# Perceiver block with 12,544 keys on one core: a dot product of the similarities moved from TensorE to VectorE, the centred input transposed in the head, hq's first half transposed sooner

## What is computed

```python
# 1: cross attention, enc = layernorm(x), decoder_hq = ctx
Sim = (enc @ w1)[:, :, None] + (ctx @ w2)[:, None, :] + einsum(enc * w3, ctx) + b_sim[0]
A = softmax(Sim, axis=2)
hq_hat = A @ ctx
Batt = softmax(max(Sim, axis=2), axis=1)
hc_bar = Batt @ enc
feats = concat([enc, hq_hat, enc * hq_hat, enc * hc_bar])
x = x + feats @ W_qv + b_qv
# 2: x = x + attn(layernorm(x))      (16 heads, rotary, no softmax)
# 3: x = x + ffn(layernorm(x))
```

## Time and profile before

| | |
|---|---|
| time of 3 runs | 112.22 us median (112.09 to 112.31) |
| the profiled execution | 112.1 us, of which 110.3 us are the span from the first to the last instruction |
| granted TensorE clock, mean over the span | 1.0 of full |
| PE busy | 105.1 us (95%), 582 matmuls |
| DVE busy | 93.1 us (84%) |
| ACT busy | 82.4 us (75%) |
| POOL busy | 29.3 us (27%) |
| DMA | 29.82 MB, mean 270 GB/s over the span |

### The profile page before, as it was taken

One profiled execution on the slowest core, in us unless ns is written; L12 is line 12 of the kernel. 1 busy time (PEld: TensorE's weight loads), 2 busy tenths in 40 slices (PEclk: granted clock), 3 DMA queues, 4 the chain that ended last, 5 costly groups with the idle time before them and its releaser, 6 DMA issues.

```text
span 110.3 us, 1855 instructions
## 1 busy us (share of the span) xinstructions
PE 105.1 (95%) x582; PEld 86.4 (78%) x583; DVE 93.1 (84%) x152; ACT 82.4 (75%) x171; POOL 29.3 (27%) x47
## 2 busy tenths in 40 slices
PE   5999999999999999999999999999999998998890
PEld 2368768588858888899899999989898997887680
DVE  1478999999998998999999999999999847674352
ACT  5067668899979989999999899988976725903450
POOL 2239200444043314233242424286330000200100
PEclk9999999999999999999999999999999999999999
DMA  2999999999999999999999999960000000000001
GB/s 72 367 406 423 416 422 422 416 422 422 409 420 417 418 415 423 417 420 442 442 389 423 415 422 425 406 260 0 3 0 0 0 6 0 0 0 0 6 3 48
DMA packets 8220, 29.82 MB, mean 270 GB/s; under 512 B 1042, under 2 KB 1298, under 8 KB 8082
## 3 DMA queue, kind: packets, MB, share of 16 engines
q1 hardware_dynamic: 8064, 29.69, 66.3%
q10 hardware_dynamic: 146, 0.01, 0.1%
HBM read 29.57 MB, written 0.13 MB: 269 GB/s over the span
## 4 chain that ended last, share of the span: by engine, by line
PE 94%; DVE 1%; issue 1%; ACT 1%; DVEq 0%; ACTq 0%
PE mixed_ps L997 18%; PE scores_ps L968 10%; PE mixed_ps L999 9%; PE scores_ps L940 8%; PE scores_ps L944 8%; PE scores_ps L954 8%; PE scores_ps L925 7%; PE scores_ps L910 4%; PE scores_ps L979 3%; PE scores_ps L1090 2%; PE mixed_ps L1142 2%; PE side_ps L1016 1%; PE scores_ps L1155 1%; PE side_ps L1133 1%; PE scores_ps L1016 1%; PE scores_ps L1125 1%
## 5 line engine op out<-in xcount | busy, mean ns | idle before, releaser
L698 DVE TENSOR_TENSOR pair<-raw,pair 128x1024 fp32r<-128x1024 f32 (+2 forms) x42 | 49.0, 1183 | 1.3 <-ACT pair L488 1.0
L488 ACT ACTIVATE pair<-raw 128x512 fp32r<-128x512 f32 (+1 forms) x42 | 34.5, 820 | 3.8 <-DMA raw<-keys_dram 3.4
L997 PE MATMUL mixed_ps<-pair,turned_high 128*128 128x512 f32 x84 | 32.3, 418 | 0.0
L999 PE MATMUL mixed_ps<-pair,turned_low 128*128 128x256 f32 x84 | 23.6, 281 | 0.0
L463 POOL CAST pair<-raw 128x512 fp32r<-128x512 f32 x22 | 13.6, 619 | 27.3 <-DVE pair L698 23.1
L997 PEld LDWEIGHTS mixed_ps<-pair,turned_high 128*128 128x128 f32 x84 | 15.8, 188 | 2.8
L520 ACT ACTIVATE turned_high<-scores_ps 128x512 fp32r<-128x512 f32 (+1 forms) x23 | 13.4, 584 | 4.0 <-PE scores_ps L968 4.0
L721 DVE TENSOR_SCALAR_CACHE_REDUCE neg_scores<-scores_ps,neg_max 128x1024 f32<-128x1024 f32 (+1 forms) x13 | 15.8, 1216 | 0.2
L999 PEld LDWEIGHTS mixed_ps<-pair,turned_low 128*128 128x128 f32 x84 | 16.0, 190 | 0.0
L728 DVE TENSOR_TENSOR turned_low<-scores_ps,turned_high 128x512 fp32r<-128x512 f32 (+1 forms) x23 | 15.3, 667 | 0.2 <-ACT turned_high L520 0.2
L968 PE MATMUL scores_ps<-ident,neg_scores 128*128 128x128 f32 x98 | 14.6, 272 | 0.0
(11 more groups left out here) (189 smaller groups left out, 130.6 us busy)
## 6 DMA issues: line engine op xcount, KB each, us to landing
raw<-keys_dram SPq DMA_DIRECT2D x24, 512.0 KB, 10.0
raw<-rows_dram SPq DMA_DIRECT2D x24, 512.0 KB, 9.2
w<-weights_dram SPq DMA_DIRECT2D x1, 1792.0 KB, 9.9
w<-weights_dram SPq DMA_DIRECT2D x2, 512.0 KB, 10.4
const<-const_dram SPq DMA_DIRECT2D x1, 832.0 KB, 11.5
raw<-keys_last_dram SPq DMA_DIRECT2D x1, 256.0 KB, 10.2
raw<-rows_last_dram SPq DMA_DIRECT2D x1, 256.0 KB, 6.8
x_sb<-x_dram SPq DMA_DIRECT2D x1, 128.0 KB, 2.2
```

What stands on the lines that cost most here:

```text
L488: nc.scalar.activation(pair[:, use % PAIR_BUFS, 0, 0:columns], raw[:, slot(item), 0:columns], ACT.Copy)\
L698: nc.vector.tensor_tensor(out=pair[:, use % PAIR_BUFS, 1, 0:columns], in0=raw[:, slot(item), 0:columns], in1=pair[:, use % PAIR_BUFS, 0, 0 ...
L997: nc.tensor.matmul(mixed_ps[:, :].rearrange("p (h d) -> p h d", h=2), probs_high, both[:, :, t * D:(t + 1) * D], start=(k == EARLY and t = ...
L999: last = nc.tensor.matmul(mixed_ps[:, 0:D], probs_low, rows_tile(high, t), start=False, stop=(k == LATE - 1 and end))
```

## The change

Three things are changed. First, `hw1` is no longer made by PE: SP loads w1 and `b_sim`, repeated in all 128 partitions (128 x 257 numbers, 1028 bytes in a row), behind chunk 14; DVE multiplies `normed` with it and sums along the row in one instruction ahead of the low half of chunk 19; `b_sim` is added in the instruction that makes `sim_max`. The small transfer of `b_sim` on ACT's queue goes. Second, ACT makes `x_c` in the head, before the query's high half; PE transposes it there (one warm-up matmul fewer), ACT copies the two halves to `x_c_t` behind the high half of chunk 3, and DVE adds `x_c_t` and the bias where x1 leaves PSUM, now for both halves; ACT squares the low half from there. Third, at the seam the first half of `hq` is transposed ahead of the last product with `normed_t` instead of behind two, the second behind it.

```diff
-WARM_START, WARM_NORM_2, WARM_SHIFT = 9, 2, 2
+WARM_START, WARM_NORM_2, WARM_SHIFT = 8, 2, 2
...
-        x_c = sb("x_c", [P, D])
+        x_c = neg_scores[:, S - 2 * D:S - D]
+        x_c_t = sb("x_c_t", [P, DH, P])
...
+        x_c_turn_ps = (banks[5][:, 0:P], banks[5][:, P:2 * P])
...
+                if k == 14:
+                    sp.dma_start(w1_rows[:, :], w1_rows_in).then_inc(w1_rows_loaded, 16)
...
-            act.dma_start(bias[:, :], bias_in).then_inc(bias_loaded, 16)
...
+            center_x()
             act.wait_ge(q_done, DH)
...
-                if k == 8:
-                    center_x()
+                if k == 3:
+                    for a in range(DH):
+                        act.wait_ge(x_c_turned, a + 1)
+                        nc.scalar.activation(x_c_t[:, a, :], x_c_turn_ps[a], ACT.Copy).then_inc(x_c_t_done, 1)
...
-            act.wait_ge(x1_projected, 1)
-            nc.scalar.activation(x1_t[:, 0, :], x1_ps[0], ACT.Identity, bias=b_c[:, 0, 0:1])\
-                .then_inc(x1_low_rows_done, 1)
-            nc.scalar.activation(x1_squared_t[:, 0, :], x1_ps[0], ACT.Square, bias=b_c[:, 0, 0:1])\
-                .then_inc(x1_low_squared, 1)
+            act.wait_ge(x1_low_rows_done, 1)
+            nc.scalar.activation(x1_squared_t[:, 0, :], x1_t[:, 0, :], ACT.Square).then_inc(x1_low_squared, 1)
...
+                    if k + 2 == 19:
+                        dve.wait_ge(w1_rows_loaded, 16)
+                        dve.wait_ge(normed_done, DH)
+                        nc.vector.scalar_tensor_tensor(hw1_parts[:, :], normed[:, :], 1.0, w1_rows[:, 0:D], ALU.mult,
+                                                       ALU.mult, accum_out=hw1_sum[:, :]).then_inc(hw1_done, 1)
                     if k + 2 < CHUNKS and not is_native(k + 2):
                         keys_low(k + 2)
...
-            nc.vector.tensor_tensor(out=sim_max[:, :], in0=hw1_ps, in1=neg_max[:, EVICTIONS:EVICTIONS + 1],
-                                    op=ALU.subtract).then_inc(sim_max_done, 1)
+            nc.vector.scalar_tensor_tensor(sim_max[:, :], hw1_sum[:, :], w1_rows[:, D:D + 1],
+                                           neg_max[:, EVICTIONS:EVICTIONS + 1], ALU.add, ALU.subtract)\
+                .then_inc(sim_max_done, 1)
...
-            dve.wait_ge(x1_projected, 2)
-            nc.vector.tensor_scalar(x1_t[:, 1, :], x1_ps[1], b_c[:, 1, 0:1], None, ALU.add)\
-                .then_inc(x1_high_rows_done, 1)
+            dve.wait_ge(b_c_done, DH)
+            dve.wait_ge(x_c_t_done, DH)
+            for a, done in ((0, x1_low_rows_done), (1, x1_high_rows_done)):
+                dve.wait_ge(x1_projected, a + 1)
+                nc.vector.scalar_tensor_tensor(x1_t[:, a, :], x1_ps[a], b_c[:, a, 0:1], x_c_t[:, a, :],
+                                               ALU.add, ALU.add).then_inc(done, 1)
...
+                if k == 5:
+                    pe.wait_ge(x_c_t_done, DH)
...
+            pe.wait_ge(x_c_done, 1)
+            for a in range(DH):
+                nc.tensor.transpose(x_c_turn_ps[a], x_c[:, a * P:(a + 1) * P], ident[:, :]).then_inc(x_c_turned, 1)
...
-                if k == 1:
-                    pe.wait_ge(ones_set, 1)
-                    pe.wait_ge(vec_loaded, 16)
-                    pe.wait_ge(bias_loaded, 16)
-                    pe.wait_ge(normed_t_done, DH)
-                    for a in range(DH):
-                        nc.tensor.matmul(hw1_ps, normed_t[:, a, :], vec[:, VC_W1 + a:VC_W1 + a + 1],
-                                         start=(a == 0), stop=False)
-                    nc.tensor.matmul(hw1_ps, ones[0:1, :], bias[0:1, 0:1],
-                                     start=False, stop=True).then_inc(hw1_done, 1)
...
-            pe.wait_ge(sim_max_done, 1)
             for k in range(EARLY, CHUNKS):
                 if k + 2 < CHUNKS:
                     turn(k + 2)
                 if k == EARLY + 1:
-
+                    pe.wait_ge(sim_max_done, 1)
...
-            pe.wait_ge(x_c_done, 1)
-            for o in range(DH):
-                nc.tensor.matmul(x1_ps[o], x_c[:, o * P:(o + 1) * P], ident[:, :], start=True, stop=False)
-            pe.wait_ge(w_combined, DH)
-            features(0, 0, normed_t)
-            for a in range(DH):
+            def turn_hq(a):
                 pe.wait_ge(hq_done, a + 1)
                 nc.tensor.transpose(hq_turn_ps[a], hq[:, a * P:(a + 1) * P], ident[:, :]).then_inc(hq_turned, 1)
-            features(0, 1, normed_t)
+
+            pe.wait_ge(w_combined, DH)
+            feature(0, 0, normed_t, 0, start=True)
+            feature(0, 0, normed_t, 1, start=True)
+            feature(0, 1, normed_t, 0)
+            turn_hq(0)
+            feature(0, 1, normed_t, 1)
+            turn_hq(1)
```

More of the change, by code:

```diff
@@ L59, with build @@
 C_MASK, C_COS, C_SIN, C_BK, C_BV, C_COS_T, C_SIN_T, C_ALL = 0, *(P + D * n for n in range(7))
-def build(nc, x, keys_in, keys_last_in, rows_in, rows_last_in, weights_in, vec_in, bias_in, const_in, out):
+def build(nc, x, keys_in, keys_last_in, rows_in, rows_last_in, weights_in, vec_in, w1_rows_in, const_in, out):
     keys_full = keys_in.rearrange("(k p) n -> k p n", p=P)
@@ L122, in build @@
         vec = sb("vec", [P, VC])
-        bias = sb("bias", [1, 1])
+        w1_rows = sb("w1_rows", [P, D + 1])
+        hw1_parts = sb("hw1_parts", [P, D])
+        hw1_sum = sb("hw1_sum", [P, 1])
         x_sb = sb("x_sb", [P, D])
@@ L237, in build @@
         vec_loaded = sem("vec_loaded")
-        bias_loaded = sem("bias_loaded")
+        w1_rows_loaded = sem("w1_rows_loaded")
         w_qv_loaded = [sem(f"w_qv_loaded{n}") for n in range(2)]
@@ L298, in build @@
         x_c_done = sem("x_c_done")
+        x_c_turned = sem("x_c_turned")
+        x_c_t_done = sem("x_c_t_done")
         w_combined = sem("w_combined")
@@ L546, in center_x @@
                 act.wait_ge(x_neg_mean_done, 1)
-                nc.scalar.activation(x_c[:, :], x_sb[:, :], ACT.Identity, bias=x_neg_mean[:, :]).then_inc(x_c_done, 1)
+                nc.scalar.activation(x_c, x_sb[:, :], ACT.Identity, bias=x_neg_mean[:, :]).then_inc(x_c_done, 1)
+            center_x()
             act.wait_ge(q_done, DH)
@@ L1011, in open_sums, with feature @@
                 nc.tensor.matmul(out_ps, idle[:, 0:P], idle[:, 0:D], start=True, stop=False)
-            def features(kind, a, source, stop=False):
-                for o in range(DH):
-                    last = nc.tensor.matmul(x1_ps[o], w[:, kind * DH + a, o * P:(o + 1) * P], source[:, a, :],
-                                            start=False, stop=stop)
-                    if stop:
-                        last.then_inc(x1_projected, 1)
+            def feature(kind, a, source, o, start=False, stop=False):
+                return nc.tensor.matmul(x1_ps[o], w[:, kind * DH + a, o * P:(o + 1) * P], source[:, a, :],
+                                        start=start, stop=stop)
             pe.wait_ge(idle_zeroed, 1)
@@ L1083, in _ @@
                 pe.wait_ge(hq_t_done, a + 1)
-                features(1, a, hq_t)
+                for o in range(DH):
+                    feature(1, a, hq_t, o)
             for a in range(DH):
                 pe.wait_ge(h_hq_done, a + 1)
-                features(2, a, h_hq_t, stop=(a == DH - 1))
+                for o in range(DH):
+                    last = feature(2, a, h_hq_t, o, stop=(a == DH - 1))
+                    if a == DH - 1:
+                        last.then_inc(x1_projected, 1)
             def project(out_ps, block_row, a):
@@ L1216 @@
         "vec": np.concatenate(columns, axis=0).T,
-        "bias": a["L0_xattn_b_sim"].reshape(1, 1),
+        "w1_rows": np.tile(np.concatenate([a["L0_xattn_w_sim"][0:D], a["L0_xattn_b_sim"]])[None], (P, 1)),
         "const": constants(a["L0_attn_bk"], a["L0_attn_bv"]),
```

11 lines of the change are left out of this document (2 added, 9 removed).

## The result

| | before | after |
|---|---|---|
| median of the runs shown together, us | 112.33 (112.09 to 113.93) | 113.69 (112.91 to 114.99) |
| profiled execution: time, span, us | 112.1, 110.3 | 113.77, 112.0 |

The changed kernel is slower: ratio 1.0109, 95% interval 1.008 to 1.0137, about 1.2 us. The forecast was slower by 0.33 us, in a range up to 112.8. The sign was right and the size was not.

A forecast was written before the change was run, and what follows sets the result against it. Bound: DMA stream up to the weights and chunk 19, then ACT, ten us of DVE, and PE from 43.5 us. Terms 0 - 0 + 0.38 - 0.05 = +0.33 us gave 112.5 us, range 112.0 to 112.8.

The forecast's parts named there:

- What bounds the kernel: Up to mix_early(0): DMA stream to weights and chunk 19, ACT, ten us of DVE, then PE from 43.5 us.
- hw1 out of PE: Before mix_early(0): PE runs 0.65 us earlier but waits there for the others; gain 0, at most 0.15 us.
- The multiply in the hole: DVE's multiply and sum for hw1 fits its wait before chunk 19's low half, at 33.08 us; cost 0.
- The transfer of w1: Behind chunk 14 in SP's queue: delays second weights part, chunk 19 and all behind by 0.38 us (0.31 to 0.5).
- The rule of the Trainium skill: For w1's 1028-byte rows: descriptors starting off 256-byte boundaries fetch unused bytes, some 36 beats instead of 32; sum 0.05 us higher.
- The head: At the start: x_c work, two transposes for one warm-up matmul, and copies are covered by waits; cost 0, otherwise 0.1 us.
- The seam: From hq to x1 and its sum of squares: PE saves 0.45 us, serial DVE leaves 0.05 us gain (0 to 0.15).
- The delay doesn't arrive: At chunk 19: an instruction load falling elsewhere removes lateness and the 0.38; -0.15 to +0.05 us, 112.1 to 112.3; chance 0.22.
- PE sets the pace: At mix_early(0) and the seam: PE is the bound, so 0.65 + 0.45 us go, 111.1; seam alone 111.8; chance 0.12.
- The new transfer is dearer: w1's transfer: rows split or one engine lags again, costing 0.8 us or more, 112.8 to 113.1; chance 0.08.

The follow-up runs named there:

- the second group: Kernel before with 32 or 128 unused bytes ahead of x_sb (113.0, 113.05 us); with raw aligned, the changed kernel (112.95) and kernel before plus unread w1 transfer (112.86).
- w1 behind the keys: Changed kernel with raw on a multiple of 256 bytes, w1 transfer issued after the last key chunk, multiply right ahead of sim_max: 112.55 us, ratio 1.0024.

## Why the prediction was wrong, point by point

- **What bounds the kernel**: right. In all profiles the distance from `mix_early(0)` to the end is 66.6 to 67.0 us, and in those of the second group it follows the arrival of chunk 20 by 9.8 us. In most of them PE's weight load waits for DVE, as "[0.17 <-DVE neg_scores L722]" above.
- **hw1 out of PE, 0**: right within what the runs can tell (113.46 with, 113.48 without, both with the transfer).
- **The multiply in the hole, 0**: right; 0.27 us of wait were left.
- **The transfer of w1, +0.38 (0.31 to 0.5)**: this step failed, and not in the length of the transfer. Its 128 packets of 1028 bytes took 47 ns each, 0.376 us of each engine, and with the tensors aligned the stream lost 0.32 to 0.36 us over it. What the step put at nothing, without a word, is the place that its destination takes: `w1_rows` and `hw1_parts` push `raw` and all behind it off the 256-byte boundary, and from about 16 us on the 4 KB packets take 163 instead of 159 ns, 2.5% more. That is 0.4 to 0.5 us up to chunk 20 in the stream, and 0.7 to 0.8 us in the medians of the kernels with a gap alone. Place and transfer together are 0.80 to 0.87 us in the stream, of a loss of 1.0 to 1.4 us in the medians of the kernels that have both. The remainder is not placed. In the profile of the changed kernel 0.61 us went before 13 us, where its packets are not slower; other kernels lost -0.1 to 0.8 there.
- **The rule of the Trainium skill that the prediction weighed** (DMA: Bandwidth & Descriptors, How a descriptor splits into AXI transactions) speaks of what begins off a 256-byte boundary. I applied it to the new rows alone, 0.05 us, and not to the neighbours that they move. For the new rows it is not borne out: 47 ns, beside 45.8 for the packets of 1024 bytes of the output, where its count, as the prediction used it, gives an estimate of 12% more. For the neighbours the runs agree with its boundary: shifts of 32 and 128 bytes cost, those of 256 do not. They do not agree with its count: by 32-byte beats a 4 KB row would cost 129 instead of 128 at 32 bytes and 132 at 128 bytes, an estimate of 0.8% and 3.1%; measured were 2.5% and 2.2% between 14 and 22 us. Nor with the start of each row as what counts, since the weights' rows did not move and were slowed too. The page's examples speak of what is fetched; here it was the SBUF side, which is written, that moved.
- **The head, 0**: not shown to be wrong. Chunk 1 was late in the profiles of the changed kernel, but also in one with the head of before (the second weights part behind chunk 20), and not in the one with head and seam alone. The head's part in what the stream loses before 13 us is open.
- **The seam, -0.05**: right in the profile (20.4 us from `hq` to the end in before, after and in the run with head and seam alone; the sum of squares 0.1 us sooner, inside the bounds of 0 and 0.15). That run's ratio of 0.9962 is 0.4 us below before, with an interval (0.9926 to 0.9997) that nearly reaches 1. No place in its profile shows where that would come from; open.
- **The rivals.** "The delay doesn't arrive" rested on the load of instructions at 28 to 30 us. With hw1 on DVE alone that load fell at 32 to 34 us and chunk 19 was as early as before, as the rival has it; but DVE then waited 0.56 us at 37.27, and `mix_early(0)` was 0.96 us late. The lag moved on and was paid there, as it was with head and seam alone (0.59 us at 36.66). "PE sets the pace" fell with w1 behind the keys: PE early, no gain. "The new transfer is dearer" came nearest in size, though 113.69 lies above its 113.1 too, and not by its mechanism: the transfer was no dearer than forecast.

## What to carry to other kernels

A new tensor has a place as well as a size. When a change allocates SBUF ahead of buffers that a saturated DMA stream writes, compute their addresses before and after; if they move by something other than a multiple of 256 bytes, price the whole stream and not the new transfer. Padding the new tensors gave the packets back here; allocating them last should do the same, which no run tried. Put a transfer whose data are needed late behind the one that the critical chain waits for.

The test was cheap and sharp: an unused gap of 32 bytes in the old kernel. To size such a cause, count how far the stream has come at two points, and take the difference: the start of one instruction in one execution mixes it with where the stream began and with which engine lagged. And before a freed engine is counted as a gain, look for the others that stand at the same point: here DVE, PE and ACT were within 0.3 us of each other at `mix_early(0)`, and DVE's own work left only the 0.47 us of wait in front of it to gain.

## What the runs showed of the hardware

- With all 16 engines busy, the 4 KB DMA packets from DRAM to SBUF took 159.0 ns each between 14 and 22 us in the kernels whose `raw` begins on a multiple of 256 bytes (whether also on one of 4096 made no difference). With `raw` and all behind it 32 or 128 bytes further they took 162.5 to 163.0 ns in the mean, 2.2 to 2.5% more.
- The packets of `w`, whose address is the same in all kernels, were slowed with the others (163.4 ns with 32 bytes, 159 without), so it is not the start of a packet's own row that decides.
- Between 8 and 12 us, in the same stream, the shift cost nothing that can be seen: 159.8 ns with 32 bytes, 159.4 before.
- Packets of 1028 bytes, at a pitch of 1028, took 47.0 ns each.
- The same program moved by such a gap alone was 0.7 to 0.8 us slower in the median (113.0 and 113.05 beside 112.26).
